# Expert weights of the soft layers: 13 loads on ScalarE's queue before the first steps, in place of SyncE's queue in steps 0 to 2

## What is computed

```python
x = L0_attn_x
x = x + _layernorm(_L0_attn_ref(_layernorm(x), Wq, bq, Wk, bk, Wv, bv, Wo, bo))        # softmax attention, 16 heads of 8
x = x + _layernorm(_L0_ffn_ref(_layernorm(x), norm1_w, norm2_w, wq, wk, wv, wo,        # attention, then a gated mixture:
        router_w, sh_gate, sh_up, sh_down, e_gate, e_up, e_down))                      # 8 experts, top 2, and a shared one
x = x + _layernorm(_L1_attn_ref(_layernorm(x), L1_attn_W))                             # power attention with decay
x = x + _layernorm(_L1_ffn_ref(_layernorm(x), router_w, router_b,                      # 7 experts with a capacity,
        experts_inter, experts_out))                                                   # and a pass-through
```

## Time and profile before

| what | value |
|---|---|
| median of three runs | 1263.33 us |
| span of the profiled execution | 1267.6 us |
| TensorE (matmul) busy | 1133.9 us, 89% |
| VectorE busy | 989.1 us, 78% |
| ScalarE busy | 853.0 us, 67% |
| GpSimd busy | 663.7 us, 52% |
| mean granted TensorE clock | 0.960 |
| soft layers in the trace | from about 15 to 509 us |

### The profile page before, as it was taken

One profiled execution on the slowest core, in us unless ns is written; L12 is line 12 of the kernel. 1 busy time (PEld: TensorE's weight loads), 2 busy tenths in 40 slices (PEclk: granted clock), 3 DMA queues, 4 the chain that ended last, 5 costly groups with the idle time before them and its releaser, 6 DMA issues. The chain is left out here.

```text
span 1267.6 us, 33680 instructions
## 1 busy us (share of the span) xinstructions
PE 1133.9 (89%) x11822; PEld 635.8 (50%) x11822; DVE 989.1 (78%) x2700; ACT 853.0 (67%) x1834; POOL 663.7 (52%) x689
## 2 busy tenths in 40 slices
PE   3879999999999997999999999789999999937876
PEld 1334444444444443466666666435566666524652
DVE  2769999999999984788988889627999999873223
ACT  1458888888888886565556556338899999733214
POOL 3214344455343320465656656527888888735763
PEclk9989999999999999999999999889999999967997
DMA  4231111111111110000000000013112111032117
GB/s 114 62 94 31 33 30 28 32 33 30 30 32 33 30 33 6 2 2 2 1 2 2 2 2 1 1 28 93 46 50 54 46 38 38 19 116 58 48 45 199
DMA packets 83140, 48.91 MB, mean 39 GB/s; under 512 B 17111, under 2 KB 80032, under 8 KB 82976
## 3 DMA queue, kind: packets, MB, share of 16 engines
q1 hardware_dynamic: 80496, 42.62, 13.0%
q0 software_dynamic: 1792, 3.70, 1.1%
q10 hardware_dynamic: 688, 0.46, 0.1%
HBM read 16.52 MB, written 10.26 MB: 21 GB/s over the span
## 5 line engine op out<-in xcount | busy, mean ns | idle before, releaser
L586 DVE TENSOR_REDUCE mxsS<-scoreS 128x2 f32<-128x512 f32 x512 | 328.6, 684 | 45.0 <-PE scoreS L694 39.8
L482 ACT ACTIVATE PTS<-stS 128x512 f32<-128x512 f32 x512 | 283.5, 591 | 58.8 <-PE stS L698 58.2
L1854 POOL TENSOR_TENSOR ghid<-gprod,ghid 128x512 f16<-128x512 f32 x144 | 165.4, 1160 | 122.8 <-ACT ghid L1967 121.2
L694 PE MATMUL scoreS<-QK 31*128 31x256 f16 x1024 | 171.9, 282 | 29.6 <-DVE mxsS L586 12.5
L894 POOL TENSOR_TENSOR PTP<-PTP,EP 128x512 f32<-128x512 f32 x128 | 162.9, 1285 | 57.8 <-ACT PTP L1073 57.6
L698 PE MATMUL stS<-QK 32*128 32x256 f16 x1024 | 168.1, 278 | 1.3 <-ACT PTS L482 1.3
L714 PE MATMUL pvS<-PTS,Vx 128*32 128x256 f32 x2048 | 140.5, 393 | 0.2
L1231 DVE TENSOR_SCALAR AP<-score_psP 128x768 int32<-128x768 int32 x128 | 121.5, 950 | 22.0 <-PE score_psP L1370 21.2
L1967 ACT ACTIVATE ghid<-gprod 128x512 f16<-128x512 f32 x144 | 90.0, 625 | 69.6 <-DVE gprod L2062 69.5
L694 PEld LDWEIGHTS scoreS<-QK 31*128 31x128 f16 x1024 | 53.2, 93 | 150.4 <-DVE mxsS L586 93.2
L1961 ACT ACTIVATE gsg<-gate_ps 128x512 f32<-128x512 f32 x144 | 84.7, 588 | 55.8 <-PE gate_ps L1904 55.2
(11 more groups left out here) (324 smaller groups left out, 2254.0 us busy)
## 6 DMA issues: line engine op xcount, KB each, us to landing
QK<-HLS SPq DMA_DIRECT2D x384, 32.0 KB, 1.9
QK<-HLP SPq DMA_DIRECT2D x192, 32.0 KB, 1.9
expert_outputs<-tzero SPq DMA_DIRECT2D x8, 512.0 KB
cgot<-expert_outputs SPq DMA_DIRECT2D x16, 256.0 KB, 5.0
tokens<-XB SPq DMA_DIRECT2D x16, 128.0 KB, 2.7
out_dram<-X SPq DMA_DIRECT2D x8, 256.0 KB, 2.3
wi<-L_ffn_experts_inter_dram SPq DMA_DIRECT2D x1, 1792.0 KB, 8.4
wo<-n_L_ffn_experts_out_dram SPq DMA_DIRECT2D x7, 256.0 KB, 3.4
```

What stands on the lines that cost most here:

```text
L482: act.activation(PT[:, n % NPT, :], st_ps[:, (NS * t + n) % 3, :], ACT.Exp, scale=SCALE).then_inc(s_exp, 1)
L586: dve.tensor_reduce(mxs[:, u // 4, :, at], score_ps[:, n % 2, :].rearrange("p (c s) -> p c s", c=TC), AX.X, ALU.max).then_inc(s_max, 1)
L694: scored = pe.matmul(score_ps[:, k, cols], QK[part, new, g, 0, rows], QK[part, new, g, 1, :], start=True, stop=True)
L1854: pool.tensor_tensor(hid[:, n // FC % NHID, 1, c, :], prod[:, n % NPROD, :], hid[:, n // FC % NHID, 0, c, :], ALU.subtract).then_inc(s_hid, 1)
```

## The change

SyncE's function `load` and its call are taken out. ScalarE gets a `load(k)` with the same 13 DMAs. It issues `load(0)` and `load(1)`, four DMAs, ahead of its first step, and `load(2)`, nine DMAs, at the start of step -1. The semaphore and the wait in step 4 stay.

```diff
-            def load(t):
-                shared = {0: "L0_ffn_sh_gate", 1: "L0_ffn_sh_up"}
-                routed = {0: "L0_ffn_e_gate", 1: "L0_ffn_e_up"}
-                if t < 0:
-                    return
-                if t < 2:
-                    sp.dma_start(experts[:, t, 0:NE, :], dram[routed[t]].rearrange("e d f -> d e f"))\
-                      .then_inc(s_experts, 16)
-                    sp.dma_start(experts[:, t, NE, :], dram[shared[t]]).then_inc(s_experts, 16)
-                elif t == 2:
-                    for e in range(NE + 1):
-                        down = dram["L0_ffn_e_down"][e] if e < NE else dram["L0_ffn_sh_down"]
-                        sp.dma_start(experts[:, 2, e, :].rearrange("p (c d) -> p c d", d=D),
-                                     down.rearrange("(c f) d -> f c d", f=P)).then_inc(s_experts, 16)
-
             for t in STEPS:
-                load(t)
                 if has(t):
                     shift(t, 1)
...
+            def load(k):
+                routed = dram[("L0_ffn_e_gate", "L0_ffn_e_up", "L0_ffn_e_down")[k]]
+                shared = dram[("L0_ffn_sh_gate", "L0_ffn_sh_up", "L0_ffn_sh_down")[k]]
+                if k < 2:
+                    act.dma_start(experts[:, k, 0:NE, :], routed.rearrange("e d f -> d e f")).then_inc(s_experts, 16)
+                    act.dma_start(experts[:, k, NE, :], shared).then_inc(s_experts, 16)
+                else:
+                    for e in range(NE + 1):
+                        down = routed[e] if e < NE else shared
+                        act.dma_start(experts[:, 2, e, :].rearrange("p (c d) -> p c d", d=D),
+                                      down.rearrange("(c f) d -> f c d", f=P)).then_inc(s_experts, 16)
+
...
+            load(0)
+            load(1)
             for t in STEPS:
                 for u in range(NU):
+                    if t == -1 and u == 0:
+                        load(2)
                     if u == 1 and has(t):
                         shifts(t, 1)
```

## The result

The median is 1259.18 us (ten executions, 1250.69 to 1264.47) against 1266.11 for the kernel before (ten executions, 1260.71 to 1270.45, the three known before the prediction among them). The ratio is 0.9937, with a 95% interval of 0.9917 to 0.9956: faster, by 0.6% and not by the 1.0% that was forecast. The profiled execution of the changed kernel spans 1257.8 us, against 1267.6. Two executions, one of the kernel before and one with the shift first, were in a slower state of the chip and are left out of all means and ratios.

What follows compares the result with a forecast made beforehand. Stages run one after another; steps 0 to 2 were long because TensorE waited for shifts behind weight loads, then ran at a lower clock. -13.5 + 0.1 + 0.1 + 0.3 = -13.0 us from 1263.3 gave 1250.3 us, range 1246.5 to 1256.

Steps and rivals of the forecast that it cites:

- The long steps are the load steps: Soft layers: steps 0, 1 and 2, where SyncE issues expert weights, are 13.47 us longer together than steps without a load.
- The shift waits for the transfer ahead of it, not for its issue: TensorE's holes at u=4, 11.32 us: the 4 KB shift arrives after 1.1 MB ahead on its queue, the greater part.
- The rest, 2.15 us, is TensorE's clock: Steps 0 to 2: beyond the holes, 2.15 us of the excess come from the clock at 0.50 after each standstill.
- -13.5 us for steps 0 to 2: Soft layers: all three steps fall to 14.13 us each without loads; bounds -14.5 and -12.5.
- The bound named for step 1: Gain can be 1 us less if SyncE's loop holds step 1, step 0's spreads having only just gone out.
- The prologue, +0.1, +0.1, +0.3: Added: 0.1 us late table load, 0.1 us transfers overlapping spreads at 15 us; 0.3 us for nine down loads at 25.8 us.
- the prediction's reading of 3.29 us: X's fourth chunk took 3.29 us to issue, read as a full queue; on ScalarE's four loads that would add 2.7 us.
- From the markers to the median: Final sum: -13.0 us taken as absolute time from the runs' median of 1263.3, giving 1250.3 us.
- B: Rival: ScalarE is held at its issues, 2.7 us at 15 us and 1.2 at 25.8; 1253.7 us, chance 0.12.
- C: Rival: bytes are paid for anyway, only 7.85 us of issue times saved, prologue spreads wait; 1255.5 us, chance 0.10.
- D: Rival: the holes at u=4 have another cause than the loads and stay; 1263 us, chance 0.05.
- E: Rival: slower, each down load holds ScalarE until landed, nine taking 20.7 us; 1268 us, chance 0.03.

Runs made afterwards that it cites:

- the shift first: From the kernel before, SyncE's load in steps 0 to 2 stands behind shift(t, 1) instead of ahead; 12.0 +- 0.7 us under before (35 executions).

## Why the prediction was wrong

Point by point, by its own steps.

**The long steps are the load steps.** Right. They are long in both profiles of before (55.9 and 55.0 us together) and 42 to 43 us together in all five of the changed kernel.

**The shift waits for the transfer ahead of it, not for its issue.** Right for steps 0 and 1, and shown by the shift placed first; the reverse in step 2. From the shift's issue to TensorE's scores it is 4.85 and 4.52 us in steps 0 and 1 of the kernel before, and 2.22 in step 2, where 1.75 is enough without a load (61.97 to 63.72 in the changed kernel). So of the lateness 3.1, 2.8 and 0.5 us are the transfer, and 1.85, 1.26 and 4.74 the issue: in step 2 the nine issues of 0.5 us each hold the shift, and their small transfers hardly do. The second profile of before has the same 4.65, 4.65 and 2.25. The reason given, that both stand in one queue, was too narrow as well: on another queue TensorE went on 5.45 us after the shift's issue.

**The rest, 2.15 us, is TensorE's clock.** Not shown as a size. With the holes gone no stretch at half clock is left in these steps, but no run takes away one without the other. In the second profile of before the holes are 1.96, 2.93 and 4.46 us, and 3.2 us of the excess are left over in place of 2.15, with 17.1 us at half clock in the three steps in place of 13.7. That fits in direction.

**-13.5 us for steps 0 to 2.** Measured 12.8, within the bounds. Step 1 is longer than the 14.13 us that were set, 14.73 to 15.19 in the five profiles, and step 0 shorter, 13.19 to 14.01. The bound named for step 1, SyncE's loop, is seen in the first profile as waits of 0.20 and 0.45 us for its DMAs. The 1 us that step 0 could give was put down to less work of earlier batches; in the profiles it goes with how early TensorE reaches full speed.

**The prologue, +0.1, +0.1, +0.3.** Measured 0.0 to 0.15 ahead of the first projection and +0.28 behind it. The four issues took 3.0 us, as counted, but not evenly: the last alone took 1.45, and the cover was just long enough. That an issue is held by a full queue is the prediction's reading of 3.29 us; no run shows what holds one. The transfers of the four, put at 0.1, cost nothing: the first spread landed in 2.0 us in both kernels. The down loads' 0.3 us was right in size and by luck; it comes by the landing of the first spreads and not by ScalarE's issues, for which it was put down.

**From the markers to the median.** This is the step that failed: "The median of the runs is 1263.33, 4.3 below that execution, and the term is in absolute time: 1263.3 - 13.0 = 1250.3." The result lies 8.9 us over it, and two things are wrong in it. The median of three executions was taken as fixed, though over ten it is 1266.11, 2.8 us higher. (The 4.3 us compare a span with a device time. Where both are on record, the span is some 2 us shorter, so the profiled execution lay about 6 us over that median; the sum didn't use this.) And 13.0 us in one stage were carried to the end as if the later stages were the same in each execution. In the comparison that counts, the difference of the medians was 6.9 us. This second one decides: from the true base a gain of 13.0 would have come out at 1253.1, within the range, while 6.9 from the assumed base gives 1256.4, just outside. Of the missing 6.1 some 0.5 are the sum's own error (12.5 for 13.0). The rest has to lie behind step 3. In the two profiled executions it can be seen: step 3 comes 13.1 us earlier (0.5 of it won ahead of the first projection, by no part of the change that is known), the end only 9.8, and 3.0 of the 3.3 us between are in the rest of the soft layers (406.8 and 409.8), with the stretch at half clock at 480 us. Rows of one and the same kernel differ there by 3 us, and by 13 in the power layer. Five comparisons together give 9.2 +- 0.7 and so leave about 3 us that are neither in the markers nor clearly chance; their cause stays open. The range of 1246.5 to 1256 had room for the terms of the sum, but none for this spread: single executions of the changed kernel lie up to 16 us apart.

**The rivals.** B (ScalarE is held) didn't come: 0.0 to 0.15 us late in place of 2.7. C (only issue time is saved) has a time, 1255.5, nearer to the result, but not its mechanism: steps 0 to 2 lost 12.8 us, more than the 7.85 us of issues. D and E are excluded: the holes are gone, and the nine issues took 5.4 us in place of 20.7.

## What to carry to other kernels

Issue the small transfer that an engine waits for ahead of the large one that nobody needs yet, or put the large one where no small one follows for its 5 us; moving it to another engine's queue in the same moment gained 1.0 +- 1.5 us. The exchange of two lines on SyncE gave 12.0 +- 0.7 us where the 13 moved loads gave 9.2 +- 0.7, and costs the prologue nothing; it is not slower, and that it is faster is not shown. Where many small loads are issued in a row, as in step 2, their issue time holds the shift, and the same exchange cures that too. A gain that is read from markers should be checked against markers: a median of a few executions carries the luck of the clock in all the stages that the change doesn't touch.

## What the runs showed of the hardware

A DMA of 4 KB issued on SyncE's queue 0.66 us after a load of 1 MB on ScalarE's was waited for until 5.45 us after its issue; the load landed 5.5 us after its own. A spread of 32 KB issued on SyncE's queue together with that load took 4.5 us to land. Behind the load on the same queue, in the kernel before, the shift was waited for until 4.85 and 4.52 us after its issue. Alone such a shift needs far less: in the changed kernel it goes out at 61.97 and TensorE's scores that wait for it start at 63.72, 1.75 us later.

The granted clock falls at other places in each execution of the same program: at 480 us in two of five profiles of the changed kernel and in one of four with the shift first, at 868 for 24 us in one of five of the changed kernel. With it the rest of the soft layers takes 406.9 to 409.8 us and the power layer 257.9 to 271.0.

Nine DMA issues on ScalarE took 5.4 us (24.92 to 30.37) where SyncE took 4.7 for the same nine. SyncE issued its spreads at the same time, 15 of them in 16.03 us where it took 15.71 before.

The last stage took 115.2 to 116.6 us in the four profiles from one chip and 107.9 to 112.4 in the others, whatever the kernel.
